# Non-local block on one Trainium2 core: theta and phi projected together with the remainders of their weights, and a new order of the stage

## What is computed

```python
theta = x @ W_theta                  # 1024 x 32
phi   = maxpool2x2(x @ W_phi)        # 256 x 32
g     = maxpool2x2(x @ W_g)          # 256 x 128
beta  = softmax(theta @ phi.T)       # 1024 x 256
out   = gamma * (beta @ g @ W_o) + x # 1024 x 256
```

## Time and profile before

| | |
|---|---|
| median of 3 runs | 239.31 us (239.09 to 239.55) |
| the profiled execution | 239.57 us, of which its span (first to last instruction) 237.7 us |
| PE busy | 232.0 us, 98% |
| PEld busy | 207.8 us, 87% |
| DVE busy | 205.3 us, 86% |
| ACT busy | 147.8 us, 62% |
| POOL busy | 167.3 us, 70% |
| DMA | 51.14 MB, mean 215 GB/s |

### The profile page before, as it was taken

The page is one execution under the profiler, slowest core; times in us unless marked ns, Lnnn a source line. Parts: engine busy times, 40 slices in busy tenths (PEclk is TensorE's granted clock), DMA queues, the critical chain, the costliest instruction groups (busy, mean ns, idle before and its releaser), DMA issues.

```text
span 237.7 us, 4361 instructions
## 1 busy us (share of the span) xinstructions
PE 232.0 (98%) x1464; PEld 207.8 (87%) x1464; DVE 205.3 (86%) x475; ACT 147.8 (62%) x274; POOL 167.3 (70%) x119
## 2 busy tenths in 40 slices
PE   7999999999999999999999999999999999999994
PEld 4777888988989899898989989898998989989794
DVE  5699988989888898988989899898988989899785
ACT  3665948577483866838477492847748385645640
POOL 1488698868679686768867677786867868642870
PEclk9999999999999999999999999999999999999999
DMA  7693029396592937739194683928659293725854
GB/s 238 220 365 128 3 70 337 130 272 258 119 374 88 337 151 242 292 105 382 60 327 191 194 341 108 343 85 289 241 150 383 61 338 139 247 107 190 318 204 181
DMA packets 14934, 51.14 MB, mean 215 GB/s; under 512 B 1856, under 2 KB 2496, under 8 KB 14912
## 3 DMA queue, kind: packets, MB, share of 16 engines
q1 hardware_dynamic: 14512, 50.67, 60.6%
q10 hardware_dynamic: 400, 0.20, 0.3%
HBM read 33.95 MB, written 16.78 MB: 213 GB/s over the span
## 4 chain that ended last, share of the span: by engine, by line
PE 89%; DMA 5%; DVE 4%; issue 1%; ACT 1%; SPq 0%; DVEq 0%
PE proj L209 23%; PE out L350 18%; PE proj L216 12%; PE proj L350 8%; PE score L255 6%; PE shift L350 6%; PE shift L310 5%; PE score L350 4%; PE score L282 4%; DMA x_t<-in_xt 2%; DMA out<-y_sb 2%; PE shift L209 1%; DVE y_sb L669 1%; DVE neg_parts L643 1%; PE score L265 1%; PE out L282 1%
## 5 line engine op out<-in xcount | busy, mean ns | idle before, releaser
L564 POOL TENSOR_TENSOR e_lo<-e_sb,e_hi 128x512 fp32r<-128x512 f32 x64 | 82.0, 1294 | 45.7 <-ACT e_sb L488 45.7
L559 POOL TENSOR_TENSOR x_lo<-x_t,x_hi 128x1024 fp32r<-128x1024 f32 x30 | 71.8, 2399 | 8.7 <-ACT x_hi L444 8.7
L485 ACT ACTIVATE e_hi<-shift 128x512 fp32r<-128x512 f32 x60 | 36.0, 600 | 17.9 <-PE shift L310 17.0
L209 PE MATMUL proj<-x_hi,w_hi 128*128 128x512 f32 x118 | 46.8, 397 | 0.1
L209 PE MATMUL proj<-x_hi,w_lo 128*128 128x512 f32 x118 | 46.6, 395 | 0.0
L643 DVE TENSOR_REDUCE neg_parts<-score 128x2 f32<-128x512 f32 x64 | 43.6, 686 | 1.1 <-PE score L255 0.2
L350 PE MATMUL out<-G_lo,e_hi 128*128 128x258 f32 x132 | 37.4, 284 | 0.0
L350 PE MATMUL out<-G_hi,e_hi 128*128 128x258 f32 x132 | 37.4, 283 | 0.0
L216 PE MATMUL proj<-x_lo,w_hi 128*128 128x512 f32 x118 | 37.3, 396 | 0.0
L350 PE MATMUL out<-G_hi,e_lo 128*128 128x258 f32 x132 | 37.2, 282 | 0.0
L488 ACT ACTIVATE e_sb<-shift 128x512 f32<-128x512 f32 x60 | 36.1, 602 | 0.0
(11 more groups left out here) (107 smaller groups left out, 480.8 us busy)
## 6 DMA issues: line engine op xcount, KB each, us to landing
x_t<-in_xt SPq DMA_DIRECT2D x32, 512.0 KB, 5.2
x_n<-in_xn SPq DMA_DIRECT2D x32, 512.0 KB, 7.6
out<-y_sb SPq DMA_DIRECT2D x31, 512.0 KB, 6.2
w_sb<-in_w_proj SPq DMA_DIRECT2D x1, 256.0 KB, 2.8
theta<-neg_hi ACTq DMA_DIRECT2D x16, 4.0 KB
theta<-neg_lo SPq DMA_DIRECT2D x16, 4.0 KB
out<-y_sb SPq DMA_DIRECT2D x1, 256.0 KB, 2.1
wo_sb<-in_w_out SPq DMA_DIRECT2D x1, 128.5 KB, 5.7
```

Source lines behind the costliest of these rows:

```text
L209: nc.tensor.matmul(bank_[:, :], w[:, c, cols:cols + P], x_hi[:, i % 2, h, c, :], start=(c == 0 and n == 0), stop=False)
L485: nc.scalar.activation(e_hi[:, i % 2, n, :], shift_bank(i, n)[:, :], ACT.Exp)
L559: nc.gpsimd.tensor_tensor(x_lo[:, i % 2, h], x_t[:, i % 2, h], x_hi[:, i % 2, h].bitcast(f32), ALU.subtract).then_inc(x_lo_ready, 1)
L564: nc.gpsimd.tensor_tensor(e_lo[:, i % 2, n, :], e_sb[:, n, :], e_hi[:, i % 2, n, :].bitcast(f32), ALU.subtract).then_inc(e_lo_ready, 1)
```

## The change

From image 3 (`PACK`) on, theta and phi are projected otherwise. A new stationary block `w_pair` holds, in its 128 columns, theta's and phi's rounded weights (64) and the remainders of the same weights (64). One matmul per chunk on `x_hi` (`pair_hi`) gives in rows 0 to 63 of the bank the product with the rounded weights, and in rows 64 to 127 the product with the remainders. `pair_lo` adds the two matmuls on `x_lo` to rows 0 to 63. ACT copies rows 64 to 127 into `corr` (`copy_corr`), and `add_corr` is one matmul with the lower half of an identity matrix (`lower`) that adds them to rows 0 to 63. So a half image takes 2 + 2 + 1 = 5 matmuls of 512 columns in place of 6. Theta now exists once, in rows 0 to 31, phi is in rows 32 to 63; the third copy of theta's rounded part, which the scores' stack needs, is made by two DMAs per image of 32 x 512 (`twin`, on SP's queue), the second part is `theta_low`'s as before. `corr`, `lower` and `w_pair` are filled once by POOL, ahead of its first `x_low`.

Beside this, the order and the banks change:
- The stage begins with `pair_hi` of both halves; `scores(b, 0)`, `pair_lo(a, 0)`, `scores(b, 1)`, `add_corr(a, 0)`, `shifted(d, 2)`, `pair_lo(a, 1)`, `scores(b, 2)`, `add_corr(a, 1)`, `shifted(d, 3)`, `values(a, 0)`, `scores(b, 3)`, `values(a, 1)` follow.
- `values` goes to banks `out0` and `out1` (from image 3 on). Output tile 0 is in `out0` still, so it now waits for `g_pool(a, 0)`; tile 3 waits for `g_pool(a, 1)`.
- `turn_max(b)` stands behind two output tiles instead of three; `shifted(b, 0)` and `shifted(b, 1)` ahead of tiles 6 and 7 instead of ahead of tile 7. This holds for stage 2 too.
- DVE: `maxima(b, 0)` first, then `phi_pool(a, 0)`, `theta_low(a, 0)`, `maxima(b, 1)`, `phi_pool(a, 1)`, `theta_low(a, 1)`, `maxima(b, 2)`, `g_pool(a, 0)`, `maxima(b, 3)`, `g_pool(a, 1)`, `phi_low(a)`.
- POOL: `g_low(a)` ahead of both `x_low(a + 1)`. In the tail `g_high`, `g_low` of the last image stand one place earlier, and `g_pool(LAST, 1)` is ahead of `neg_low(LAST)`.

The core of the diff:

```diff
+        def phi_max(i):
+            return outb[1][THETA:P, 0:NK] if i < PACK else proj[0][PAIR:THETA, 0:NK]
         def value_bank(i, h):
-            return shift[h] if i < 2 else proj[h]
+            return shift[h] if i < 2 else proj[h] if i == 2 else outb[h]
...
-            return (outb[0], outb[1], proj[0], proj[1], shift[0], outb[0], outb[1], score[1])[t]
+            if i < LAST - 2:
+                return (outb[0], proj[1], shift[0], outb[1], proj[0], score[1], outb[0], outb[1])[t]
...
+            def pair_hi(i, h):
...
+                pe.wait_ge(x_hi_ready, 2 * i + h)
+                for c in range(CC):
+                    last = nc.tensor.matmul(proj[h][:, :], w_pair[:, c, :], x_hi[:, i % 2, h, c, :],
+                                            start=(c == 0), stop=(c == CC - 1), skip_group_check=True)
+                last.then_inc(corr_ready, 1)
+            def pair_lo(i, h):
+                pe.wait_ge(x_lo_ready, 2 * i + h + 1)
+                for c in range(CC):
+                    nc.tensor.matmul(proj[h][0:PAIR, :], w_pair[:, c, 0:PAIR], x_lo[:, i % 2, h, c, :],
+                                     start=False, stop=False, skip_group_check=True)
+            def add_corr(i, h):
...
+                pe.wait_ge(corr_copied, packed(i, h))
+                nc.tensor.matmul(proj[h][0:PAIR, :], lower[:, :], corr[:, h, :],
+                                 start=False, stop=True, skip_group_check=True).then_inc(tp_ready, 1)
...
+                elif t == 0:
+                    pe.wait_ge(g_pooled, 2 * later + 1)
...
+                elif t == 3:
+                    pe.wait_ge(g_pooled, 2 * later + 2)
...
                 if s > 2:
-                    for h in range(2):
-                        theta_phi(a, h)
-                        scores(b, h)
-                        shifted(d, 2 + h)
-                    for h in range(2):
-                        values(a, h)
-                        scores(b, 2 + h)
+                    pair_hi(a, 0)
+                    pair_hi(a, 1)
+                    scores(b, 0)
+                    pair_lo(a, 0)
+                    scores(b, 1)
+                    add_corr(a, 0)
+                    shifted(d, 2)
+                    pair_lo(a, 1)
+                    scores(b, 2)
+                    add_corr(a, 1)
+                    shifted(d, 3)
+                    values(a, 0)
+                    scores(b, 3)
+                    values(a, 1)
                 if a < LAST:
-                    outputs(d, (0, 1, 2))
+                    outputs(d, (0, 1))
                     turn_max(b)
-                    outputs(d, (3, 4))
+                    outputs(d, (2, 3, 4))
                     mix(a)
-                    outputs(d, (5, 6))
+                    output(d, 5)
                     shifted(b, 0)
                     shifted(b, 1)
-                    output(d, 7)
+                    outputs(d, (6, 7))
...
+            def copy_corr(i, h):
+                act.wait_ge(corr_ready, packed(i, h))
+                nc.scalar.copy(corr[PAIR:P, h, :], proj[h][PAIR:P, :]).then_inc(corr_copied, 1)
...
+            def twin(i, h):
+                pixels = slice(HALF * h, HALF * (h + 1))
+                sp.wait_ge(theta_hi_ready, 2 * i + h + 1)
+                sp.dma_start(theta[2 * DK:THETA, i % 3, pixels].bitcast(f32),
+                             theta[0:DK, i % 3, pixels].bitcast(f32)).then_inc(theta_twin[i % 3][h], 16)
...
+            nc.gpsimd.memset(corr[0:PAIR, :, :].bitcast(f32), 0.0).then_inc(corr_zero, 1)
...
+            nc.gpsimd.tensor_copy(lower[:, :], ident[:, PAIR:P]).then_inc(lower_ready, 1)
...
+            nc.gpsimd.tensor_copy(w_pair[:, :, 0:PAIR], w_hi[:, :, PAIR:P].bitcast(f32)).then_inc(w_pair_ready, 1)
+            nc.gpsimd.tensor_copy(w_pair[:, :, PAIR:P], w_lo[:, :, PAIR:P].bitcast(f32)).then_inc(w_pair_ready, 1)
```

More of the change, by code:

```diff
@@ L19 @@
 GW = C + 2
+PAIR = 2 * DK
 PROJ = P + DV
+PACK = 3
 WARM = 8
@@ L44, in nonlocal_block @@
         w_hi, w_lo = sb("w_hi", [P, CC, PROJ], f32r), sb("w_lo", [P, CC, PROJ], f32r)
+        w_pair = sb("w_pair", [P, CC, P], f32r)
+        lower = sb("lower", [P, PAIR], f32r)
+        corr = sb("corr", [P, 2, HALF], f32r)
         wo_sb, w_og = sb("wo_sb", [P, C + 1]), sb("w_og", [P, C])
@@ L97, in nonlocal_block @@
         w_hi_ready, w_lo_ready = sem("w_hi_ready"), sem("w_lo_ready")
+        w_pair_ready, lower_ready, corr_zero = sem("w_pair_ready"), sem("lower_ready"), sem("corr_zero")
+        corr_ready, corr_copied = sem("corr_ready"), sem("corr_copied")
+        theta_twin = [[sem(f"theta_twin{s}{h}") for h in range(2)] for s in range(3)]
         wog_ready, wo_hi_ready, wo_lo_ready = sem("wog_ready"), sem("wo_hi_ready"), sem("wo_lo_ready")
@@ L122, in neg_loads, with twins, packed @@
             return 32 * (i // 3 + 1)
+        def twins(i):
+            return 16 * (i // 3)
+        def packed(i, h):
+            return 2 * (i - PACK) + h + 1
         def max_row(i, r):
@@ L163, in _ @@
                 a, b, d = s, s - 1, s - 2
+                if a >= PACK:
+                    for h in range(2):
+                        twin(a, h)
                 max_into_stack(b)
@@ L171, in _ @@
                 store(d, 1)
+            for h in range(2):
+                twin(LAST, h)
             max_into_stack(LAST - 1)
@@ L248, in scores @@
                         pe.wait_ge(neg_lo_ready, i)
-                    if i > 1 and i < LAST:
-                        pe.wait_ge(y_ready, TILES * (i - 2) + TILES)
+                    if 2 < i < LAST:
+                        pe.wait_ge(y_ready, TILES * (i - 2) + 6)
                 else:
@@ L519, in _ @@
                 if s > 2:
-                    for h in range(2):
-                        theta_high(a, h)
-                        exps(d, 2 + h)
+                    copy_corr(a, 0)
+                    copy_corr(a, 1)
+                    theta_high(a, 0)
+                    exps(d, 2)
+                    theta_high(a, 1)
+                    exps(d, 3)
                     phi_high(a)
@@ L538, in _ @@
             neg_high(LAST)
+            g_high(LAST)
             exps(LAST - 1, 3)
-            g_high(LAST)
             exps(LAST, 0)
@@ L590, in _ @@
                 e_low(d, 3)
-                if a == 2:
+                if a < LAST:
                     g_low(a)
                     x_low(a + 1, 0)
-                    x_low(a + 1, 1)
-                elif a < LAST:
-                    x_low(a + 1, 0)
-                    g_low(a)
                     x_low(a + 1, 1)
@@ L601, in _ @@
             e_low(LAST - 1, 2)
+            g_low(LAST)
             e_low(LAST - 1, 3)
-            g_low(LAST)
             for n in range(4):
@@ L732, in _ @@
                 if s > 2:
-                    for h in range(2):
-                        phi_pool(a, h)
-                        theta_low(a, h)
-                        maxima(b, h)
-                    phi_low(a)
+                    maxima(b, 0)
+                    phi_pool(a, 0)
+                    theta_low(a, 0)
+                    maxima(b, 1)
+                    phi_pool(a, 1)
+                    theta_low(a, 1)
+                    maxima(b, 2)
                     g_pool(a, 0)
-                    maxima(b, 2)
+                    maxima(b, 3)
                     if a < LAST:
                         g_pool(a, 1)
-                    maxima(b, 3)
+                    phi_low(a)
                 if a < LAST:
@@ L757, in _ @@
             maxima(LAST, 3)
-            finishes(LAST - 2, (5, 6, 7))
+            finishes(LAST - 2, (5, 6))
+            g_pool(LAST, 1)
             neg_low(LAST)
-            g_pool(LAST, 1)
+            finishes(LAST - 2, (7,))
             finishes(LAST - 1, (0, 1, 2, 3, 4))
```

114 lines of the change are left out of this document (71 added, 43 removed).

## The result

The changed kernel takes 246.66 us (median of 4 runs, 245.84 to 248.22); the kernel before, measured beside it, took 239.43. The ratio is 1.0295, with a 95% interval of 1.0225 to 1.0365: slower. The forecast was 244.5, range 241.0 to 248.0. A program like this has a second, slower state in some executions; ratios and intervals leave these out, while a median is over all runs, so a ratio need not be the quotient of the two medians.

The account below looks back on a forecast made before the run. TensorE's stream was taken as the bound. 4.8 (tile 0's wait less matmuls saved) + 0.45 (start) + 0.7 (stage 2) - 0.7 (tail) = +5.2 on the profiled 239.57, 244.8; less 0.26 to the median, 244.5 us, range 241.0 to 248.0.

Parts of the forecast that it names:

- The bound and the matmuls removed: TensorE's stream bounds stages of 14.09 us; 26 matmuls fewer at 0.234 take 6.1 us off it.
- The wait at tile 0: Tile 0 waits 0.84 for `g_pool(a, 0)`; stage 14.46, 0.37 longer, 13 times: +4.8 us.
- Its three steps: Stage start to `phi_pool(a, 0)` 2.30; VectorE's chain to `g_pool(a, 0)` 4.24; VectorE's end to TensorE's weight load 0.06.
- Work costed at nothing: `copy_corr` on ACT, twins, `g_low` and other moved work cost 0; if tile 0's wait went, `turn_max` is late next.
- the same 3 us: The maxima's DMA has 3 us between `neg_low` and `shifted(b, 0)`, as before; no cost.
- The rule set against the rows: On VectorE the place written counts as well as the place read, so no step of the chain gets shorter.
- The rival that only the place read counts: VectorE's two steps from `theta_low` to `maxima` take 0.60: 2.9 less in all, 241.6 us; 8%.
- the one that the chain overlaps: VectorE's five steps beside 32-row instructions overlap, chain 0.58 shorter, 7.5 less: 237.0 us; 8%.
- The third, ACT late: `copy_corr(a, 0)` ends at 2.3 instead of 1.26, the chain 0.4 later: 5.2 more, 249.7 us; 8%.
- The start: POOL's fills take 1.3 to 2.2 ahead of `x_low(1, 0)`, about 1.4 in idle time: +0.45 on TensorE's path.
- Stage 2: `turn_max(1)` stands behind two tiles instead of three and waits longer for `maxima(1, 3)`: +0.7.
- The tail: The last image's `mix` no longer waits for `g_lo`: -0.7, or nothing if a DMA takes the wait's place.

Follow-up runs that it names:

- Experiment 6: The kernel of experiment 5 with the first matmul of `pair_hi` issued twice, so 6 matmuls per half image again: 243.12 us, ratio 1.0137.
- experiment 11: Experiment 10's kernel with ACT's order put back (`g_high` ahead of `neg_high`), `neg_low` still ahead of the first `finish`: 233.96 us, ratio 0.9759.
- experiment 1: The changed kernel with the banks of output tiles 0 and 1 exchanged for images 1 to 12: 237.67 us, ratio 0.9901.
- experiment 7: The changed kernel without the two `twin` DMAs per image and TensorE's waits for them: 246.69 us, ratio 1.0295.
- experiment 5: The changed kernel with the edits of experiment 1, experiment 2 and Experiment 3, and POOL's fills ahead of its wait for `W_o`: 236.73 us, ratio 0.9859.
- experiment 4: The changed kernel with POOL's fills ahead of its wait for `W_o`, and `turn_max(1)` behind three tiles again in stage 2: 246.40 us, ratio 1.0296.
- Experiment 3: The changed kernel with two buffers for `y_sb`, so no `finish` waits for the store of the image before: 245.87 us, ratio 1.0264.
- experiment 2: The changed kernel with `g_pool(a, 0)` ahead of `maxima(b, 2)` on VectorE: 239.83 us, ratio 0.9995.
- experiment 12: Experiment 5 with only two tail edits: `neg_low(LAST)` ahead of `g_pool(LAST, 1)`, the last maxima's DMA ahead of the load: 235.78 us, ratio 0.9829.
- experiment 9: Experiment 5 with `neg_high` ahead of `g_high` on ACT, `neg_low` ahead of the first `finish`, and `neg_low(LAST)` ahead of `g_pool(LAST, 1)`: 240.08 us, ratio 1.0018.
- experiment 10: Experiment 9 with the last maxima's DMA issued ahead of the load of `x_n(LAST, 0)` on SP: 240.22 us, ratio 1.0005.

## Why the prediction was right, and where it was off

**The bound and the matmuls removed: right.** Stages of 14.09 with nothing waiting, 26 x 0.234 = 6.1 to be had. Experiment 6 gives 6.4 for the same 26 (with two stages that waited for a DMA), experiment 11 stages shorter by 0.47.

**The wait at tile 0: right in place, cause and size.** Its three steps came out as read from the kernel before: 2.31 for 2.30, 4.22 for 4.24, 0.07 for 0.06. A stage lasts 14.487 for 14.46. The prediction's own steps come closer than the figure it went on with: they add up to tile 0 at 7.40, a wait of 0.86 and a stage of 14.48. The 7.38 and 0.84 ("Rounded for the readings") have no row behind them, and that difference is 0.2 of the 0.3 by which the twelve stages were forecast too low. The stages make 4.76 of the 7.15, the largest part of the loss, and experiment 1, which only puts one tile in front of the wait, makes the kernel faster than before.

**Work costed at nothing: right.** `copy_corr` ends 1.75 into the stage for 1.8, the twins cost nothing (experiment 7), no added wait but tile 0's shows in a stage. What would be late next if tile 0's wait went was named wrongly: not `turn_max`, but the maxima's DMA in front of `shifted(b, 0)`. The prediction had given it "the same 3 us" as before. Experiments 1 and 5 show that it has no margin once the stage is 13.7.

**The rule set against the rows: right.** The pair that no row before had, `theta_low` (reads from row 0, writes from row 32) and then `maxima`, stands 0.71 and 0.72 apart, with nothing waited for, while two instructions on 128 rows stand 0.60 apart. And it is not that the instruction covers few rows. `neg_low`, on 8 rows from row 0 on, holds nothing back: the next starts 0.07 before its listed end. From VectorE's timeline of the changed kernel:

```profile
226.80 0.27 DVE L743 TENSOR_TENSOR neg_lo<-score,neg_hi 8x128 fp32r<-8x128 f32 x1
227.00 0.15 DVE L753 RECIPROCAL r_sum<-proj 128x1 f32<-128x1 f32 x1
```

So the place written holds too. This is what the Trainium skill states (VectorE: DVE Perf Modes, section "Two Vector instructions with no wait between them"), and the trace agrees. The sentence that the prediction set against it, from the section "The DRAIN you can't avoid" of the same page, is limited in that section itself: the Trainium skill adds there that an instruction which is not held starts earlier. So the 0.60 speaks against neither section. The rival that only the place read counts (241.6 us) is refuted by these rows, and so is the one that the chain overlaps (237.0). The third, ACT late (249.7), is refuted by ScalarE's timeline, and no wait for a copy is listed.

**The start: the term of +0.45 did not show.** The fills took 1.6, within the 1.3 to 2.2. POOL's idle time of 1.4, against which I held them, is no constant: it lies between the landing of `W_o` and the end of `x_high(1, 0)`, and in this execution `W_o` landed 0.8 earlier than before. Tile 0 of stage 2 stands at 28.25, before at 28.42. In experiment 1, where `W_o` landed later, the fills cost about 0.2 (experiment 4). How far the start's misses are chance can't be told from one execution.

**Stage 2: right**, +0.63 for +0.7.

**The tail: the term that failed.** The sum had -0.7 for the last `mix`, with the condition "if a DMA takes the wait's place, this is nothing". A DMA did, and cost more than that: with +0.37 for tile 0's last wait, the tail should have been 0.33 shorter and was 1.68 longer. Experiment 3 takes 1.67 of these 2.0 back in the profiled execution. The rest is about what `mix` still waits, 0.4, now for a `finish` (last line of the list of waits above), and that `finish` is the one that waited for the store of 6.01. What made the store take 5.08 in place of 3.1 was not found: it is not the twins, since without them the wait is 1.8 still. A `finish` of image 15 waits 1.6 to 2.2 for a store in each version of the changed kernel with one buffer (experiments 1, 2, 4 and 7), so it is no accident of one execution; in the medians its price is 0.5 to 0.8.

Start and tail together were 1.3 too low, the stages 0.3, the time outside the span 0.25: that makes 244.8 to 246.7. The start was forecast 0.7 too high and so hid a third of the tail's 2.0; that part of the close result is luck.

## What to carry to other kernels

When tiles move to other banks, list for each bank who reads it last and where that reader stands in its own engine's order, and sum start-to-start distances from the stage's start up to it; an engine that has time left (VectorE is busy 85%) can hold the busiest one this way. Work saved on the bounding engine counts in full only while the first consumer of a reused bank is not next in line: here one tile of other work in front of it was worth 9 us (246.66 and 237.67). When moving an instruction to the front, move its DMA issue along in the account: it occupies its engine's order although the page does not count it.

## What the runs showed of the hardware that was not expected

- In experiment 5 a DMA of 4 KB issued by SP landed 1.84 us after its issue in the steady stages, and 3.1 in the tail, 3.5 us behind a load of 512 KB. In experiment 12, ahead of that load, it was 2.4 from issue to use.
- In the runs without tile 0's wait of 0.84 the same stages were 0.4 to 1.3 longer for that DMA: stage 13 in experiments 1, 2, 5, 12 (14.25 or 14.26 each), stage 4 in 11, both in 6. Experiments 9 and 10, in which 2.9 lie between the DMA's issue and its use, have no such stage. In experiment 5 the view of the DMA queues from 184.0 to 186.5 (queue and kind, packets, MB, share), and the wait of `shifted(12, 0)` behind it:

```profile
q14 instruction: 1, 0.01, 0.9%
```
```profile
186.46 0.73 PE L371 MATMUL shift<-theta,phi 98*128 98x512 f32 x2 [0.35 <-DMA theta<-neg_lo]
```

  The maxima's DMA, issued at 184.09, took 2.37 in place of 1.84. A transfer of the kind "instruction" falls in this window, and in those of the other long stages; the stage before (170.3 to 172.8) has none. But stage 4 of experiments 5 and 12 has one as well, and is not longer. Whether the one causes the other was not tried and stays open.
- Issuing such a DMA from ScalarE held up its next instruction by 0.66 us (experiment 9).
- Stores of 512 KB, of one size and layout, landed after 2.6 to 8.0 us in one execution of the changed kernel, and after 2.6 to 6.0 in its tail.
- The start of stage 3 lay between 35.9 and 37.9 us in executions of kernels with almost the same start. So a gain below 1 us at the start can't be read from one profiled execution, and the stages' lengths, which apart from the long ones repeat to 0.07 within an execution, are the better measure.
